# A graph network with one-hot adjacency blocks: the last four output tiles behind a flag branch, and the encoder without a block left out

## The reference, cut to what matters

```python
edge_index = jnp.stack([src, dst])               # 53125 edges between 3125 nodes, sorted by dst
h = jnp.maximum(_layernorm(x, axis=-1), 0.0)     # x is 3125 x 128
x = x + _L0_gnn_ref(h, edge_index, ...)
h = jnp.maximum(_layernorm(x, axis=-1), 0.0)
x = x + _L1_gnn_ref(h, edge_index, ...)

def _L0_gnn_ref(x, edge_index, ...):
    h = jnp.maximum(x @ enc_w1.T + enc_b1, 0.0) @ enc_w2.T + enc_b2
    def step(h, w):                               # five layers
        m = h @ w
        agg = jax.ops.segment_sum(m[src], dst, num_segments=n_nodes)
        ...                                       # a GRU cell of agg and h
    h, _ = jax.lax.scan(step, h, conv_w)
    h = jnp.maximum(h, 0.0)
    out = jnp.maximum(h @ dec_w1.T + dec_b1, 0.0) @ dec_w2.T + dec_b2
    return jax.nn.sigmoid(out)

def _L1_gnn_ref(x, edge_index, W1, b1, W2, b2):
    row, col, v = _norm_adj(n, edge_index)        # v = deg[row]**-0.5 * deg[col]**-0.5
    h = _spmm(row, col, v, x, n)
    h = jax.nn.relu(h @ W1.T + b1)
    h = _spmm(row, col, v, h, n)
    return h @ W2.T + b2
```

## Time and profile before

| | |
|---|---|
| median of three runs | 745.32 us (745.05 to 745.38) |
| the profiled execution | 745.62 us, of which 743.3 us are the span of the trace |
| TensorE (PE) busy | 721.4 us, 97% |
| VectorE (DVE) busy | 335.2 us, 45% |
| ScalarE (ACT) busy | 315.2 us, 42% |
| GpSimd (POOL) busy | 44.5 us, 6% |

### The profile page before, as it was taken

One profiled execution on the slowest core, in us unless ns is written; L12 is line 12 of the kernel. 1 busy time (PEld: TensorE's weight loads), 2 busy tenths in 40 slices (PEclk: granted clock), 3 DMA queues, 4 the chain that ended last, 5 costly groups with the idle time before them and its releaser, 6 DMA issues.

```text
span 743.3 us, 9918 instructions
## 1 busy us (share of the span) xinstructions
PE 721.4 (97%) x4071; PEld 394.4 (53%) x4071; DVE 335.2 (45%) x677; ACT 315.2 (42%) x463; POOL 44.5 (6%) x56
## 2 busy tenths in 40 slices
PE   6889999999999999999999999999999999999997
PEld 3556666445444444444444444444445545558886
DVE  7999999525023241123231223646644631123432
ACT  3977877645344344234452334432447421212000
POOL 4240000000000000000000000120002210000000
PEclk9999999999999999999999999999999999999999
DMA  5020000734102332022230212710002000000100
GB/s 164 6 84 16 4 2 5 147 69 81 9 1 55 63 51 46 1 48 39 53 75 0 49 37 38 115 63 2 1 0 97 9 1 1 1 1 6 34 31 25
DMA packets 79240, 28.41 MB, mean 38 GB/s; under 512 B 70519, under 2 KB 78390, under 8 KB 79062
## 3 DMA queue, kind: packets, MB, share of 16 engines
q1 hardware_dynamic: 78230, 26.93, 17.2%
q0 software_dynamic: 240, 0.66, 0.3%
q10 hardware_dynamic: 720, 0.13, 0.1%
HBM read 8.03 MB, written 2.60 MB: 14 GB/s over the span
## 4 chain that ended last, share of the span: by engine, by line
PE 85%; DVE 9%; ACT 2%; DMA 2%; POOL 1%; issue 1%; SPq 0%; DVEq 0%; ACTq 0%; POOLq 0%
PE PSA L1241 35%; PE PSA L1458 9%; PE PSA L1323 7%; PE PSA L1402 5%; PE PSA L1186 4%; PE PSA L1254 3%; PE PSA L1263 3%; PE PSA L1258 3%; PE PSA L1262 3%; PE PSA L1256 3%; PE PSA L1265 3%; DVE CT L869 3%; PE PSA L1390 2%; PE PSA L1378 1%; DMA H<-yS 1%; DVE stat L834 1%
## 5 line engine op out<-in xcount | busy, mean ns | idle before, releaser
L1241 PE MATMUL PSA<-AT,H 128*128 128x512 fp8e3 (+1 forms) x1470 | 275.8, 347 | 0.8 <-DMA H<-yS 0.8
L1241 PEld LDWEIGHTS PSA<-AT,H 128*128 128x128 f16 x1470 | 126.8, 98 | 151.9 <-issue 12.0
L1078 DVE SCALAR_TENSOR_TENSOR rS<-PSA,bias,rS 128x512 f32<-128x512 f32 (+1 forms) x35 | 23.9, 682 | 261.6 <-ACT rS L1635 261.6
L1635 ACT ACTIVATE rS<-PSA,bias 128x512 f32<-128x512 f32 (+1 forms) x35 | 22.1, 632 | 199.6 <-PE PSA L1262 199.6
L869 DVE TENSOR_TENSOR CT<-CT 128x2048 bf16<-128x2048 bf16 x80 | 91.4, 1206 | 0.0
L1565 ACT ACTIVATE AT<-PSA 128x1000 fp8e3<-128x1000 f32 (+1 forms) x79 | 74.4, 997 | 20.7 <-PE PSA L1186 20.5
L1539 ACT ACTIVATE CTL<-AT 128x3125 fp8e3<-128x3125 fp8e3 (+1 forms) x25 | 69.9, 2797 | 0.0
L1402 PE MATMUL PSA<-CT,H 128*128 128x512 fp8e3 (+1 forms) x336 | 65.5, 351 | 0.3 <-POOL H L762 0.3
L1458 PE MATMUL PSA<-AT,CT 128*128 128x256 f16 x576 | 65.1, 273 | 0.6 <-DVE AT L1040 0.6
L1458 PEld LDWEIGHTS PSA<-AT,CT 128*128 128x128 fp8e3 x576 | 55.4, 98 | 7.2 <-DVE AT L1040 0.8
L1323 PE MATMUL PSA<-AT,H 128*128 128x512 fp8e3 x245 | 58.0, 379 | 1.2 <-ACT AT L1565 1.2
(11 more groups left out here) (181 smaller groups left out, 661.8 us busy)
## 6 DMA issues: line engine op xcount, KB each, us to landing
AT<-scale_scratch SPq DMA_DIRECT2D x1, 1562.5 KB, 6.5
H<-in_x SPq DMA_DIRECT2D x1, 1536.0 KB
out<-AT SPq DMA_DIRECT2D x12, 128.0 KB
comb_scratch<-CT SPq DMA_DIRECT2D x1, 960.0 KB, 4.5
comb<-comb_scratch SPq DMA_DIRECT2D x5, 192.0 KB, 2.5
H<-yS SPq DMA_TRANSPOSE x48, 2.5
H<-in_x SPq DMA_DIRECT2D x1, 512.0 KB, 4.9
CT<-AT SPq DMA_TRANSPOSE x25, 4.0
```

The lines of the kernel that those rows point to most:

```text
L1241: last = nc.tensor.matmul(bank[:, 0:w], H16[:, l % 2, t, h, :], AT3[:, t, n0:n0 + w], start=(t == 0 and h == 0), stop=(t == T - 1))
```

## The change

Four things are changed, and two small ones beside them.

1. FLAGGED = 20: the last four output tiles on TensorE and VectorE stand behind the flag's branch, once in the branch for the general path and once in its Else. SyncE, ScalarE and GpSimd keep their order.
2. `step(b)` leaves no block out: encoder steps 8 to 15 stand at blocks 7 to 14, before at 8 to 15, and with them the norms. PART is timed anew up to block 22.
3. Chunks 4, 5 and 6 are normalized by ScalarE, behind its encoder step of blocks 6, 8 and 10; VectorE only makes their shifts.
4. GpSimd writes a ramp of 128 f32 (`lanes`) in place of `iotaP`, and ScalarE spreads it into `iotaP`.

Beside these the second warm-up matmul has 256 columns in place of 384, and one semaphore is merged into another.

```diff
+        FLAGGED = 20
-        REST = 7
-        step = lambda b: b - ENC - (b > REST) if b != REST else None
+        BY_SCALAR = (0, 1, 4, 5, 6)
+        BY_VECTOR = (2, 3)
+        step = lambda b: b - ENC
-        PART = {7: [(0, 0, 4)], 8: [(0, 4, 8)], 10: [(0, 8, 12)], 12: [(0, 12, 16)], 13: [(1, 0, 4)], 14: [(0, 16, 20)],
...
+        PART = {7: [(0, 0, 4)], 8: [(0, 4, 8)], 9: [(0, 8, 12)], 11: [(0, 12, 16)], 13: [(0, 16, 20)], 14: [(1, 0, 4)],
...
-            pool.iota(iotaP, [[1, 128], [0, 2]], base=0, channel_multiplier=0,
-                      allow_small_or_imprecise_dtypes=True).then_inc(onehot_iotas, 1)
+            pool.iota(lanes, [[1, 128]], base=0, channel_multiplier=0,
+                      allow_small_or_imprecise_dtypes=True).then_inc(lanes_numbered, 1)
...
                     if b == block_of[2 * n_] - 2:
                         first_norm(n_)
                     if b == block_of[2 * n_] - 1:
-                        normalized(n_)
+                        shifts(n_) if n_ in BY_SCALAR else normalized(n_)
...
+            def output_tile(u):
+
+                bank = PS[TILES[u % STARTED]]
+                dve.wait_ge(sum2_ready, u + 1)
+                link(nc.vector.scalar_tensor_tensor(OUT[:, u, :], bank[:, 0:F], dinvO[:, u:u + 1], X32[:, u, :],
+                                                    ALU.mult, ALU.add))
+                nc.vector.scalar_tensor_tensor(OUT[:, u, :], bank[:, F:2 * F], dinvO[:, u:u + 1], OUT[:, u, :],
+                                               ALU.mult, ALU.add).then_inc(output_ready, 1)
...
             with dve.If(dve.value_load(flag[0:1, 0:1], min_val=0, max_val=1000) > 0):
+                for u in range(FLAGGED, 2 * FG):
+                    output_tile(u)
                 general_vector(dve)
+            n[0] = chained
+            with dve.Else():
+                for u in range(FLAGGED, 2 * FG):
+                    output_tile(u)
...
-            for n in (512, 384):
+            for n in (512, 256):
...
+                    if s in BY_SCALAR:
+                        pe.wait_ge(tile_normalized, BY_SCALAR.index(s) + 1)
+                    else:
+                        pe.wait_ge(later_normalized, BY_VECTOR.index(s) + 1)
...
+            for u in range(STARTED, FLAGGED):
+                next_tile(u)
...
             with pe.If(pe.value_load(flag[0:1, 0:1], min_val=0, max_val=1000) > 0):
+                for u in range(FLAGGED, 2 * FG):
+                    next_tile(u)
                 general_tensor(pe)
+            with pe.Else():
+                for u in range(FLAGGED, 2 * FG):
+                    next_tile(u)
...
+            act.wait_ge(lanes_numbered, 1)
+            nc.scalar.activation(iotaP, lanes.unsqueeze(2).to_broadcast([SL, 128, 2]), ACT.Copy).then_inc(onehot_iotas, 1)
             act.wait_ge(samples_loaded, 32)
...
+                for s in BY_SCALAR[2:]:
+                    if b == block_of[2 * s] - 1:
+                        normalized(s)
```

More of the change, by code:

```diff
@@ L173, in gnn_kernel @@
         kf = early([PW, KW, SL], F32)
+        lanes = tf[:, KW - 1, :]
         pkT = early([SL, 2, KW * PW], BF16)
@@ L247, in gnn_kernel @@
         assert all(b + 1 < k * (PW // J) for b, k in KEYS_AT.items())
-        PART = {7: [(0, 0, 4)], 8: [(0, 4, 8)], 10: [(0, 8, 12)], 12: [(0, 12, 16)], 13: [(1, 0, 4)], 14: [(0, 16, 20)],
-                15: [(1, 4, 8)], 16: [(0, 20, 24)], 17: [(1, 8, 11)], 18: [(0, 24, T), (1, 11, 13)]}
-        PART.update({19 + i: [(1, 13 + 3 * i, 16 + 3 * i)] for i in range(4)})
+        PART = {7: [(0, 0, 4)], 8: [(0, 4, 8)], 9: [(0, 8, 12)], 11: [(0, 12, 16)], 13: [(0, 16, 20)], 14: [(1, 0, 4)],
+                15: [(0, 20, 24)], 16: [(1, 4, 8)], 17: [(0, 24, T), (1, 8, 10)]}
+        PART.update({18 + i: [(1, 10 + 3 * i, 13 + 3 * i)] for i in range(5)})
         EVEN = [0, 4, 7, 11, 14, 18, 21, T]
@@ L271, in gnn_kernel @@
         keys_ready = sem("keys_ready"); keys_transposed = sem("keys_transposed")
-        keys_copied = sem("keys_copied"); onehot_iotas = sem("onehot_iotas")
+        keys_copied = sem("keys_copied"); onehot_iotas = sem("onehot_iotas"); lanes_numbered = sem("lanes_numbered")
         onehots_ready = sem("onehots_ready"); windows_counted = sem("windows_counted")
@@ L276, in gnn_kernel @@
         ident_set = sem("ident_set"); gate_biases = sem("gate_biases")
[L277 removed]
+        weights_loaded = sem("weights_loaded"); combined_loaded = sem("combined_loaded"); encoder_loaded = sem("encoder_loaded")
         weights2_loaded = sem("weights2_loaded"); x_loaded = [sem("x_loaded0"), sem("x_loaded1")]; x_reloaded = sem("x_reloaded")
@@ L705, in _ @@
             pool.memset(last_start, float(E - SL)).then_inc(steps_set, 1)
-            pool.memset(mhalf[:, :], -0.5).then_inc(mhalf_set, 1)
+            pool.memset(mhalf[:, :], -0.5).then_inc(steps_set, 1)
             pool.memset(ident[:, :], 0.0).then_inc(ident_set, 1)
@@ L732, in _ @@
             gathered(1)
-            pool.wait_ge(mhalf_set, 1)
+            pool.wait_ge(steps_set, 3)
             roots(0)
@@ L1033, in decoded_tail @@
                         biased_output(c)
-                for u in range(2 * FG):
-                    bank = PS[TILES[u % STARTED]]
-                    dve.wait_ge(sum2_ready, u + 1)
-                    link(nc.vector.scalar_tensor_tensor(OUT[:, u, :], bank[:, 0:F], dinvO[:, u:u + 1], X32[:, u, :],
-                                                        ALU.mult, ALU.add))
-                    nc.vector.scalar_tensor_tensor(OUT[:, u, :], bank[:, F:2 * F], dinvO[:, u:u + 1], OUT[:, u, :],
-                                                   ALU.mult, ALU.add).then_inc(output_ready, 1)
+                for u in range(FLAGGED):
+                    output_tile(u)
                     if u == CHECKED:
@@ L1151, in _ @@
             dve.wait_ge(flag_ready, 1)
+            chained = n[0]
             with dve.If(dve.value_load(flag[0:1, 0:1], min_val=0, max_val=1000) > 0):
+                for u in range(FLAGGED, 2 * FG):
+                    output_tile(u)
                 general_vector(dve)
+            n[0] = chained
+            with dve.Else():
+                for u in range(FLAGGED, 2 * FG):
+                    output_tile(u)
         @block.tensor
@@ L1201, in encoder @@
                     t0, nt = CH[s]
-                    pe.wait_ge(tile_normalized, s + 1) if s < 2 else pe.wait_ge(later_normalized, s - 1)
+                    if s in BY_SCALAR:
+                        pe.wait_ge(tile_normalized, BY_SCALAR.index(s) + 1)
+                    else:
+                        pe.wait_ge(later_normalized, BY_VECTOR.index(s) + 1)
                     if s >= 1:
@@ L1485, in _, with next_tile @@
                 tile_ends(u)
-            for u in range(STARTED, 2 * FG):
+            def next_tile(u):
                 pe.wait_ge(output_ready, u - STARTED + 1)
@@ L1579, in normalized @@
                 t0, nt = CH[s]
-                act.wait_ge(shifts_ready, s + 1)
+                act.wait_ge(shifts_ready, BY_SCALAR.index(s) + 1)
                 for t in range(t0, t0 + nt):
@@ L1647, in _ @@
             act.dma_start(ends_i, row_ends).then_inc(row_ends_loaded, 16)
-            act.wait_ge(mhalf_set, 1)
+            act.wait_ge(steps_set, 3)
             nc.scalar.activation(flag_f[0:1, 0:1], mhalf[0:1, 0:1], ACT.Copy)
```

1 line of the change is left out of this document (removed).

## The result

The changed kernel took **748.51 us** in the median of seven runs (747.37 to 751.33), the kernel before 745.32 (744.95 to 745.64): a ratio of 1.0045, 95% interval 1.0035 to 1.0055. It is slower. The forecast was 747.5 with 744.9 to 749.4; the sign and the range held, and the middle was 1.0 us short. The runs also spread over 4 us, where those of the kernel before lie within 0.7.

The account below looks back on a forecast made before the run. TensorE, busy 97% of the span, was taken to bound the kernel. From the profiled 745.62 us, start -0.4, blocks +1.4 and tail +1.2 gave 747.8, as a median 747.5 us, range 744.9 to 749.4.

Parts of the forecast that it names:

- start: Startup: narrower ramp and ScalarE's spreading let the counting matmuls start near 4.5 us, not 4.96; -0.4 us.
- blocks 5 to 8, idle time: TensorE's waits there: longer at block 6, one for ScalarE's normalizing at block 7, none at block 8; +0.7 us.
- blocks 9 to 12: TensorE's waits for VectorE's one-hots ahead of blocks 9 and 11, about 1.15 us where block 10 had 1.2; -0.1 us.
- block 13: The product needing ScalarE's copied keys stands sooner in the block, so TensorE waits longer for them; +0.8 us.
- gap at tile 20: TensorE's flag and jump, moved behind tile 19, hold tile 20 until about 730.6 us; +2.9 us.
- end of the span: VectorE's far jump no longer ends the span; SyncE's chain does, 2.28 us behind VectorE's last output; -1.65 us.
- time around the span: Profiled execution outside its span, 2.3 us in the kernel before, taken as unchanged; 0.
- rival 3: The clock falls in the gap ahead of tile 20, so about one tile runs at half speed; +1.9 us, 749.4, chance 0.14.
- the tail: Last four output tiles and end: TensorE's added gap less the saving behind VectorE's last output; +1.2 us.
- the same (0.26 + 0.14): Outcome of no telling change, 743.8 to 746.8 us; 0.26 from a rival with blocks near 0, 0.14 from the forecast's low part.
- Rival 2: TensorE's jump ahead of tile 20 is hidden, the tail gives -1.65 us; faster, 743.6 us, chance 0.11.

Follow-up runs that it names:

- t_pe: Kernel before, with the flag ahead of the last four output tiles on TensorE alone, VectorE reading it at its end: 749.67 us, ratio 1.0058.
- t_both: Kernel before, with only the tail's part of the change, the last four output tiles behind the flag on TensorE and VectorE: 746.18 us, ratio 1.0020.
- t_dve: Kernel before, with the flag ahead of the last four output tiles on VectorE alone, TensorE reading it at its end: 742.95 us, ratio 0.9973.
- swap13: blocks_only, with block 13's aggregate piece put ahead of the encoder product that waits for the copied keys: 744.84 us, ratio 0.9997 to the kernel before.
- swap_norm: swap13, with chunk 4's statistics behind the one-hots of block 6 again, as in the kernel before: 743.43 us, ratio 0.9978.
- pe_near: t_dve, with TensorE's flag also ahead of the last four tiles but its condition turned round so the fast path falls through: 743.24 us, ratio 0.9975.
- start_dve: Kernel before, with the change's startup part and the flag ahead of the last four tiles on VectorE alone: 743.21 us, ratio 0.9973.
- blocks_only: Kernel before, with only the block phase's part of the change (steps, PART, norms by ScalarE), start and tail as before: 747.62 us, ratio 1.0040.
- filled13: blocks_only, with two extra TensorE matmuls that the result doesn't need in block 13's pause: 746.50 us, ratio 1.0024 to the kernel before.

## Why the prediction was right, and what it missed

The number came out inside the range, and its places are the right ones; that the middle lay only 1.0 us off is in part luck, as the runs show below. Point by point, with the terms as forecast and as the profile and the runs have them:

| term | forecast | measured |
|---|---|---|
| start | -0.4 | -0.4 in the profile; not to be told from 0 in the medians |
| blocks 5 to 8, idle time | +0.7 | +0.75 (3.07 to 3.82) |
| blocks 9 to 12 | -0.1 | -0.4 (1.06 to 0.64) |
| block 13 | +0.8 | +0.9 (1.19 to 2.13) |
| gap at tile 20 | +2.9 | +2.89 in the profile; +4.6 where the clock falls (t_pe) |
| end of the span | -1.65 | -1.69 |
| time around the span | 0 | -0.2 in the profile; -0.4 in t_both and t_dve |
| clock | 0 (rival 3: +1.9, at the tail only) | +1.7 at block 13 in the profile; 1.8 in the upper group of t_both |

The mechanism was right in each of its places: which waits go, which come, that TensorE's jump is laid bare and VectorE's taken off the end. The mis-sized term is the clock. The prediction had it as a rival with a chance of 0.14, in the tail's gap alone, and took from the earlier trace rows that it falls about 3.0 us after the array runs dry, so that the waits of 2 us in the blocks were counted at their own length. The runs showed in its place that it falls for pauses of 2.0 to 2.7 us too, in some executions and not in others: behind the 1.96 us of block 13 in the profile of the changed kernel, behind the 2.08 of block 6 in that of swap13 and not in the changed kernel's, behind 2.73 in the profile of t_pe and, by their times, in its other four runs, behind the gap at tile 20 in five of t_both's eleven. Nor does it wait for 3.0 us of standing array. Worked out from the mean over the stretch in which it fell, as the prediction did, it fell 2.2 us after the array ran dry in the changed kernel (0.52 from 66 to 67, so at 66.04; dry at 63.82), 2.9 us in t_pe (0.62 from 730.1 to 731, so at 730.32; dry at 727.46) and 3.4 us in swap13 (0.62 from 38 to 39, so at 38.24; dry at 34.82); in all three the array was at work again by then. Each fall cost 0.4 us at block 6 in swap13's profile, where a later wait takes up part of it, 0.9 to 1.0 in the upper group of swap13 if that is the same fall, and 1.7 to 1.8 elsewhere. The pauses of up to 1.6 us in the blocks of swap_norm came without it: its eleven runs lie within 0.5 us.

The spread of the changed kernel fits with falls that differ from run to run, but not so that its runs at 747.4 to 747.7 are the forecast's kernel without a fall. Their mean granted clocks are 0.997, 0.998 and 0.998, as in the profiled run (0.998, with one fall seen); of the other three, 748.51 has 0.998, 748.60 has 0.990, and the slowest, 751.33, has 0.993. Kernels with VectorE's new tail and no long pause in the blocks (t_dve, pe_near, start_dve) read 0.992 to 0.993 or 1.000. By this six of the seven had at least one fall, and for the slowest 0.993 means either none or about three; its time speaks for the latter. Which falls each run had was not seen.

The kernel without a fall would then lie under the forecast's 747.5. I estimate 746.5 to 747.0, from the parts: 745.3 of before, nothing for the start, +0.5 for the tail (t_both's lower group), and for the blocks +0.75 (the profiled run of blocks_only less the 1.7 of its fall) to +1.2 (filled13's lower group). The forecast had -0.4, +1.2 and +1.4 for the three. So it was 0.5 to 1.0 too high in what it counted, 0.4 of which is the time around the span, and it left out the clock at 1.7 or more; the two errors cancel in part.

Two slips of the working stand beside this. By the prediction's own parts the chances come to 0.40 for the same (0.26 + 0.14) and 0.49 for slower (0.35 + 0.14), where it gave 0.29 and 0.61. And the pace of a tile is 2.68 us, from first matmul to first matmul (730.40 - 727.72); the 2.66 ran from a first to a last one. Neither moves the forecast.

The Trainium skill (TensorE: Matmul & The Clock Gate, Part 1: The HAM clock gate) describes the gate as running freely, so that where a pause lies against it differs from run to run; the trace agrees, in that one and the same pause of 2.08 us was followed by 0.56 of the clock in one kernel and by 1.00 in another. By this reading the prediction's argument "it fell 3.0 us after" took a single row for a rule.

Rival 2, that the jump would be hidden, was wrong for its reason: with 3.85 us the jump is as long in the middle of the work as at the end. The runs settle that it is the jump and not the load, the checks or the place: with all of these the same it is 86 ns when it falls through. That it is the distance is not varied by itself. For it speaks that the jumps of SyncE and ScalarE in the kernel before, taken as well, take 63 and 50 ns and their next instruction is at most 0.5 us later; how far they go was not compared. The Trainium skill (Runtime: NRT & Kernel Launch, Instruction fetch mechanics) says of a branch out of the fetched pages what the prediction drew on; the trace of pe_near agrees, with its 86 ns for a branch that isn't taken, but no run here shows the fetch itself.

VectorE's part alone gave 2.2 us and not the 1.7 that its profile shows in the span. The time around the span was 1.8 in t_dve and 2.3 in the profiled execution of before; what makes it differ between programs stays open (it was 1.9 in blocks_only and 2.3 in t_pe, which both have VectorE's old tail). Whether blocks 9 to 12 gained 0.3 more than forecast by ScalarE's share or by PART's new times was not tried apart.

## What to carry to other kernels

A branch to the end of the program, 3.1 to 3.9 us here, is cheap where an engine with slack takes it, and dear in the middle of the bounding engine's stream: move it on the engine that has slack, and where it must stand in the stream, let the likely path fall through. On a kernel bound by TensorE, price a pause like those here (1.96 to 2.73 us) not at its length alone but with a chance of 0.4 to 1.8 us of lost clock behind it; put a piece of independent work into it (filled13, swap13), or split it (swap_norm). And where single runs of a change form two groups, compare their mean granted clocks before blaming the measurement.
